# Weighted passes of a graph kernel: stored adjacency blocks replaced by stored source one-hots and a mark per slot

## What is computed

```python
def _sage_conv(x, src, dst, ea, Wl, bl, Wr):
    msg = relu(x[src] + ea)                                  # ea: edge attributes, 64 wide
    s = segment_sum(msg, dst, num_segments=N)
    cnt = segment_sum(ones, dst, num_segments=N)
    return s / maximum(cnt, 1.0)[:, None] @ Wl + bl + x @ Wr  # three of these in a row
...
def _wgin_layer(x, src, dst, edge_weight, W1, W2):
    agg = segment_sum(edge_weight[:, None] * x[src], dst, num_segments=N)
    return relu(agg @ W1.T) @ W2.T                            # two of these in a row
```

## Time and profile before

| | us |
|---|---|
| time before, median of 3 runs | 13441.07 (13429.87 to 13461.34) |
| span of the profiled execution | 17899.9 |
| first pass in it (122 to 4256) | 4134 |
| second, third pass (4367 to 5841, 5880 to 7350) | 1474, 1470 |
| weighted passes (7423 to 8222, 8277 to 9075) | 799, 798 |
| attention layers and dense parts (the rest) | about 9200 |

### The profile page before, as it was taken

How to read it: one execution, slowest core, us unless ns; L and a number is a source line. 1 busy time by engine, 2 the same in 40 slices (tenths; PEclk the granted TensorE clock), 3 DMA queues, 4 the chain that set the end, 5 groups by cost and what they waited for, 6 DMA issues and landing times. The chain is left out here.

```text
span 17899.9 us, 289186 instructions
## 1 busy us (share of the span) xinstructions
PE 11230.3 (63%) x73051; PEld 9956.4 (56%) x73052; DVE 8110.3 (45%) x22787; ACT 4549.9 (25%) x9519; POOL 8237.8 (46%) x8516
## 2 busy tenths in 40 slices
PE   5777777777878788687854444554444454455454
PEld 4666666765777677576744444443444443444443
DVE  4444444444333333300045555554555555555556
ACT  2333333333111111100012332332323232233333
POOL 3333333332444444333425555545555553555553
PEclk8777776677777777798965555555555555555555
DMA  3444444443444444465622232222222232233321
GB/s 120 136 132 132 132 134 134 134 134 101 128 122 125 116 123 123 130 209 167 210 72 71 71 72 71 74 60 62 70 71 71 70 73 51 70 74 74 72 73 48
DMA packets 1390391, 1840.09 MB, mean 103 GB/s; under 512 B 402712, under 2 KB 1116467, under 8 KB 1388954
## 3 DMA queue, kind: packets, MB, share of 16 engines
q1 hardware_dynamic: 749274, 832.66, 15.3%
q10 hardware_dynamic: 367424, 691.34, 11.8%
q0 software_dynamic: 272384, 301.97, 9.4%
HBM read 1408.99 MB, written 416.01 MB: 102 GB/s over the span
## 5 line engine op out<-in xcount | busy, mean ns | idle before, releaser
L2027 POOL DMA_INDIRECT rows<-gat_table,idx x2457 | 2357.8, 960 | 2331.1 <-DMA idx<-in_src 1527.6
L2027 POOL DMA_INDIRECT Y<-gat_table,idx x2394 | 2299.3, 960 | 1715.4 <-DMA idx<-in_src 901.5
L2059 PE MATMUL bank<-ident,scratch 8*128 8x8 f32 x1386 | 388.9, 352 | 3519.5 <-DVE scratch L2166 2249.0
L881 POOL DMA_INDIRECT bins<-scratch,slots x1288 | 1283.6, 997 | 2457.9 <-DVE slots L1146 1136.3
L2059 PEld LDWEIGHTS bank<-ident,scratch 8*128 8x128 f32 x1386 | 343.6, 306 | 3722.9 <-issue 3722.9
L893 POOL DMA_INDIRECT rows<-node_table,idx x1386 | 1361.8, 983 | 1707.6 <-DMA idx<-in_src 1316.9
L947 PE MATMUL bank<-xT 112*64 112x120 f32 (+1 forms) x11648 | 1831.9, 333 | 131.5 <-issue 130.5
L947 PEld LDWEIGHTS bank<-xT 112*64 112x64 f32 (+1 forms) x11648 | 1741.2, 183 | 179.6 <-issue 158.9
L1237 ACT ACTIVATE xT<-xT 112x256 f32<-112x256 f32 x1456 | 603.9, 415 | 3839.5 <-DVE xT L1074 2623.1
L1074 DVE TENSOR_TENSOR xT<-scores,xT 112x256 f32<-112x256 f32 x1028 | 435.0, 423 | 2431.2 <-remote 1496.7
L2086 PE MATMUL bank<-sel,msg 128*72 128x32 f32 x9702 | 1308.6, 309 | 0.0
(11 more groups left out here) (249 smaller groups left out, 21346.7 us busy)
## 6 DMA issues: line engine op xcount, KB each, us to landing
work<-in_dst_rows SPq DMA_DIRECT2D x693, 448.0 KB
work<-near_table SPq DMA_DIRECT2D x858, 224.0 KB
xT<-bins ACTq DMA_DIRECT2D x1456, 119.0 KB
adj<-work ACTq DMA_DIRECT2D x598, 240.0 KB
work<-adj ACTq DMA_DIRECT2D x184, 780.0 KB
xT<-adj ACTq DMA_DIRECT2D x184, 780.0 KB
near_table<-work SPq DMA_DIRECT2D x598, 224.0 KB
bins<-zeros ACTq DMA_DIRECT2D x46, 1547.0 KB, 7.8
```

The source lines that it names most:

```text
L881: nc.gpsimd.indirect_dma_start(bins, bass.IndirectOffsetOnAxis(slots[u % 2][:, r * G + j:r * G + j + 1], 0), binf[r][:, j, :], None).then_ ...
L2027: nc.gpsimd.indirect_dma_start(rows[s][:, j, :], None, gat_table, bass.IndirectOffsetOnAxis(idx[s % RR][:, j:j + 1], 0)).then_inc(s_rows[s ...
L2059: nc.tensor.matmul(small[:, 64:64 + H], spread_out[:, 0, :], ident[0:H, 0:H], start=True, stop=True)
```

## The change

The weighted passes no longer use adjacency blocks. `gin_pass` is gone, `sage_pass` is now `cell_pass`, and the weighted passes are `cell_pass(…, NBK, 1, weighted=True)`: they load the stored `near` (13 pieces of 224 KB per block, SP queue), fetch the node rows by it, multiply them by the weight of the slot on DVE (`weigh`), make `far_hot` on DVE, and sum by destination, with the bursts after pieces 3, 7 and 12. ACT does nothing in them. Destination place and weight of each slot come from a new small DRAM tensor `mark_table`, which the first pass fills: one ACT copy of 8 columns per piece (`mark`) and one store of 46 KB per block. The first pass loses `turned_cells`, its `weigh`, `adjacency` and `keep`, and its fetch gets the freed PSUM bank 4 as a second one.

```diff
-        adj = dram("adj", (NBK, P, TS * MW))
+        mark_table = dram("mark_table", (NBK, SL, TS * 2))
...
+        marks = [sb(f"marks{i}", [P, TS * 2]) for i in range(2)]
+        marked = [m[0:SL, :].rearrange("p (t v) -> p t v", v=2) for m in marks]
...
-            at_plain = [5] if first_pass else [1, 5, 9]
+            at_plain = [5] if first_pass else [1] if weighted else [1, 5, 9]
...
-            joint = [bank[3]] if first_pass else [bank[3], bank[4]]
+            joint = [bank[3], bank[4]]
...
+                    def marks_load(b, u):
+                        wait(sp, (q["joined"], NPC * (b - 1)))
+                        sp.dma_start(marks[u % 2][0:SL, :], mark_table[ds(b, 1), :, :].rearrange("o p f -> (o p) f")
+                                     ).then_inc(s_marks[u % 2].handle, 16)
...
-                    def adjacency(b, u, i):
-
-                        qn, k = NPC * b + i, NPC * u + i
-                        wait(pe, (q["weighed"], qn + 1), (q["far_hot_ready"], qn + 1), (q["adj_out_ready"], qn))
-                        for c in range(PC):
-                            last = nc.tensor.matmul(adj_sum[:, c * MW:(c + 1) * MW], turned[k % R][0:SL, c * P:(c + 1) * P],
-                                                    far_hot[k % RR][0:SL, c * MW:(c + 1) * MW], start=True, stop=True)
-                        last.then_inc(q["adj_ready"].handle, 1)
...
-                        wait(pe, (q["cells_ready"], qn + 1), (q["far_hot_ready"], qn + 1),
+                        wait(pe, (q["joined" if weighted else "cells_ready"], qn + 1), (q["far_hot_ready"], qn + 1),
...
+                    def weigh(qn, k, s, u, i):
+                        wait(ve, (q["fetched"], qn + 1), (q["cells_summed"], qn - RR + 1))
+                        nc.vector.tensor_tensor(cellf[s][0:SL, :, 0:D], joint[k % JR][0:SL, 0:PC * D].rearrange("p (c d) -> p c d", d=D),
+                                                bc(marked[u % 2][:, i * PC:(i + 1) * PC, 1], [SL, PC, D], 2), ALU.mult).then_inc(q["joined"].handle, 1)
...
-                    def turned_cells(qn, k, s):
-                        wait(ve, (q["adj_ready"], qn - R + 1))
-                        nc.vector.tensor_tensor(turned[k % R][0:SL, :].rearrange("p (c m) -> p c m", m=P), bc(counts[0:SL, 1:P + 1], [SL, PC, P], 1),
-                                                bc(payf[s][0:SL, :, D], [SL, PC, P], 2), ALU.is_equal).then_inc(q["turned_ready"].handle, 1)
...
-                        for c in range(PC):
-                            w = turned[k % R][0:SL, c * P:(c + 1) * P]
-                            last = nc.scalar.activation(w, w, ACT.Copy, scale=payf[s][0:SL, c, D + 2:D + 3])
-                        last.then_inc(q["weighed"].handle, 1)
...
-                        nc.scalar.activation(adj_out[s], adj_sum[:, 0:PC * MW], ACT.Copy).then_inc(q["adj_out_ready"].handle, 1)
-                        wait(ac, (q["adj_out_ready"], qn + 1))
-                        ac.dma_start(adj[ds(b, 1), :, i * PC * MW:(i + 1) * PC * MW].rearrange("o p f -> (o p) f"), adj_out[s]).then_inc(s_kept[s].handle, 16)
+                    def mark(qn, s, b, u, i):
+                        if i == 0:
+                            wait(ac, (s_marks_kept[u % 2], 16 * (b // 2) if isinstance(b, int) else 8 * (b - u % 2)))
+                        nc.scalar.activation(marked[u % 2][:, i * PC:(i + 1) * PC, :], payf[s][0:SL, :, D + 1:D + 3], ACT.Copy).then_inc(q["marked"].handle, 1)
...
-        gin_pass("gin0", node_table, X)
+        cell_pass("gin0", node_table, X, NBK, 1, weighted=True)
```

More of the change, by code:

```diff
@@ L850, in body @@
                                     aux_load(b, u, it, at_aux.index(i))
+                            if weighted and i == 3 and not (isinstance(b, int) and b == B - 1):
+                                marks_load(*after(b, u, it, 1)[:2])
                             if i in at_plain and not (isinstance(b, int) and b == B - 1):
@@ L1271, in body @@
                             if first_pass:
-                                weigh(qn, k, s)
-                                if i > 1:
-                                    keep(b, u, it, i - 2)
-                                elif not (isinstance(b, int) and b == 0):
-                                    keep(*after(b, u, it, -1), NPC + i - 2)
+                                mark(qn, s, b, u, i)
                             if not (isinstance(b, int) and qn + RR >= pieces):
                                 cells_load(*spot(b, u, it, i, RR))
+                        if first_pass:
+                            marks_keep(b, u)
                     if first_pass:
@@ L1317, in sage_pass @@
                 overflow()
-            sum_further(name, table, True, first_pass)
+            sum_further(name, table, not weighted, first_pass)
         def overflow():
```

205 lines of the change are left out of this document (59 added, 146 removed).

## The result

The changed kernel takes 13945.9 us (median of four runs, 13943.1 to 13948.0), the kernel before, timed beside it, 13435.5 us (13413.0 to 13461.3). The ratio is 1.0385, 95% interval 1.0372 to 1.0397: slower, by 510 us.

What follows compares the result with a forecast made beforehand. PE's order, with the adjacency in it, was taken to pace the first pass; 17899.9 + 1910 - 1191 = 18619 us profiled, +719 x 0.7509 = +540, a median of 13980 us; range 13420 to 14700.

Steps and rivals of the forecast that it cites:

- The weighted passes: Fetches and sums priced by the second pass: 38.1 us per block, 1754 us per pass, 1910 us added by two.
- The warm bound: Weighted-pass block at a granted clock of 1.00: 29.2 us, or 1342 us per pass.
- No stage with fetches has had over 0.78: Argument against the clock staying up in the new weighted passes, which would give 13362 us.
- The first pass: Loses the adjacency products, 971.8 us, and half the idle time before them, 220: gains 1191 us, down to 2943 us.
- my bounds of 408 and 1777: First-pass gain: 408.1 us if DVE's order paces it, 1777 us if adjacency work and both PE waits all go.
- The even factor: Conversion of the profiled execution to the median, 13441.07 / 17899.9 = 0.7509, used on all stages: +719 becomes +540 us.
- the rival of the uneven scale: Old weighted passes keep 797 us unprofiled, the rest shrinks by 0.7265: median 13527 us; chance 0.14.
- The clock falls: Clock of 0.5 in the new weighted passes and the first pass: median 15294 us; chance 0.07.
- The clock stays up: New weighted passes at 1342 us each add 1086 us, less than the first pass gives: 13362 us; chance 0.07.
- The first pass down to POOL: First pass falls until POOL is full, 44.0 us per block, gaining 2111 us: median 13290 us; chance 0.06.
- The loads don't keep up: In the weighted passes PE would wait for `near_table` before fetches; priced inside the upper bound, no chance of its own.
- PE's idle time put down to `weigh`: Sign in the weighted passes: PE's idle time before the fetch would be put down to DVE's `weigh`.

Runs made afterwards that it cites:

- before_look: The kernel before the change, without an edit, run in the slow place for a profile: 18191.3 us.
- double_fetch: The changed kernel with each fetch product of the first pass made twice, in the quick place: 14092.8 us, ratio 1.0499 to the kernel before.
- turned_back: The changed kernel with DVE's comparison of the old first pass put back, its result unused, in the slow place: 18741.9 us, ratio 1.0446 to the kernel before.
- two_adj: The kernel before with two alternating PSUM banks for the first pass's adjacency products, one for its fetch, in the quick place: 13150.8 us, ratio 0.9791.
- second_bank: The kernel before with a second PSUM bank for the fetch of its first pass, in the quick place: 13431.2 us, ratio 1.0.

## Why the prediction was right, and where its steps were off

The forecast was 13980 us; the time is 13945.9. The direction and the mechanism hold: the weighted passes add more than the first pass gives. That the total is only 34 us off is luck: both terms are far off, and their errors cancel.

**The weighted passes: right mechanism, term too large.** Forecast 1754 us each in the slow place, measured 1460 and 1480. Per block that is 31.7 us against 38.1. PE's part is 1247.5 / 46 = 27.1 us where I had 32.3, idle time 4.6 us where I had 5.8. The step that failed is the price of a product: I took it from the second pass, at a clock of 0.78, and the new passes ran at 0.86 and 0.85. A sum costs 295 ns in them and not 330, a fetch 283 and not 300. The added time was 1317 us and not 1910. The warm bound, 29.2 us per block, was no bound for the quick place: there a block takes 25.1 us, 24.3 of them PE busy at a clock of 0.96, and of the 5.8 us idle time less than 1 is left. "No stage with fetches has had over 0.78" was true of the one trace that I had, and fell by the other place, where the second pass has 0.97.

**The first pass: right mechanism, term too large as well.** Forecast 2943 us, measured 3451 in the slow place, a gain of 739 and not 1191. Three steps make up the 452 us. The first is a reading: I took the whole 971.8 us of the adjacency products off PE's busy time, though their records overlap with others'. By the trace of `before_look` PE is busy 2315 of its 3143 us with products other than these, so their removal takes 828 us and not 972 (144 us). The second is the price of what stays: 2315 us became 2537.5 (223 us), by a factor of 1.10, and the clock fell from 0.71 to 0.64, by 1.11; a fetch takes 350 ns after, 321 before. The third is idle time: it fell by 133 us, 1047 to 914, where I had half of the wait before the adjacency products, 220 (86 us). `double_fetch` shows the same link from the other side, products put back into this pass raise its clock. The gain lies between my bounds of 408 and 1777, and the pass stayed just under the 3500 us from which I had called DVE's order the bound; `turned_back` says that DVE's comparison is paid at 154 to 208 of 408 us. I had PE's order as what paces this pass: for the kernel before `two_adj` bears that out, but after the change `double_fetch` speaks against it.

**The sum and its conversion.** In the slow place both terms came short, by 452 and 593 us: +578 by stages for a forecast of +719. Converted evenly by 0.7509 the terms were -894 and +1434, +540 in sum; in the quick place -549 and +1061 came, and +510 in the medians, so that errors of 345 and 373 us cancel there. The even factor is wrong stage by stage. From the slow to the quick place the first pass shrinks to 0.71, the second to 0.66, a weighted pass to 0.77 before and 0.79 after. So the rival of the uneven scale was right that the scale is uneven, and wrong in what it did with it: it kept the old weighted passes at 797 us (625 measured) and shrank all the rest by 0.7265, the new ones to 1274 us (1154 measured). What I called "a profiled execution" against "the median" was in truth one place against another.

**The other rivals.** *The clock falls* came true in the first pass (to 0.64 in the slow place, 0.80 against 0.84 in the quick one) and not in the weighted passes, where it stayed near that of the old ones (0.88 and 0.86 in the slow place, 0.98 and 0.96 in the quick one); what stays in the first pass cost 223 us more, not thousands. The Trainium skill (TensorE: Matmul & The Clock Gate, "HAM oscillation — how this bites in real kernels") has an array that waits between bursts of products fall back to the throttled clock. The first pass agrees with it in direction: products went, most of the idle time stayed (1047 us before, 914 after), and the clock fell from 0.71 to 0.64. The weighted passes have 4.6 us idle per block and stayed at 0.86. *The clock stays up* was right on the clock of the weighted passes in the quick place (0.96), but its gain was not to be had: converted as it was, it had them add 1086 x 0.7509 = 815 us, and 1061 came, while the first pass gained only 549. *The first pass down to POOL* did not happen in the slow place, where a block takes 75.0 us. In the quick place it takes 52.9, not far above POOL's own work, which by this rival's count (busy time and the time from one DMA to the next) is 2162 / 46 = 47.0 us. *The loads don't keep up* is refuted by 14.4 us before the fetch.

**What the profile after was to show.** PE idle before the fetch of the first pass below 585 us: 88 in the slow place, 0 in the quick one. Fetches and sums each over 600 us busy: 643 and 616 in the slow place, 595 and 539 in the quick one, so this was a sign for one place only. A clock of 0.75 to 0.85: 0.85 and 0.86 in the slow place, 0.96 in the quick one, so just above it or well above it. A first pass near 2940 us: no, 3451 in the slow place, and 2434 in the quick one where 2943 x 0.7509 = 2210 would be its like. PE's idle time put down to `weigh`: wrong in the quick place (7 us), in part right in the slow one (64.5 of 216.9 us before the fetches). `near_table` below 50 us: yes. Weighted passes not below 1394 us each: 1460 and 1480 in the slow place; the 1154 us of the quick one are to be held against 1394 x 0.7509 = 1047.

**Still open.** Why one place is slower. Single instructions take the same time in both: the destination one-hots (L1069, later L1063) 651 and 649 ns, ACT's copy for relu some 0.41 us, and the DMA queue of the loads 2728 us of packets (15.0% of 18190) and 2740 (20.4% of 13431) for the same 832.66 MB. Longer are the waits, and the granted clock is lower (0.76 against 0.97 in the second pass). The clock can't be the whole cause: in the attention layers it is 0.50 in both places, a product by `ident` takes 424 ns in both, and yet 8200 us of `before_look` (9300 to 17500) hold 4529 records of it where 6300 us of `second_bank` (6700 to 13000) hold 4641, 1.33 times the time for each. What is longer there is idle time, in part such as no releaser ends: 296 us of it before one group on DVE (L2188, `work<-scores,work`) against 6. Where that comes from stays open. The 418 us of the first pass that neither the bank nor the comparison explains are not split further either.

## What to carry to other kernels

Price products by the clock that the stage will have after the edit, not by the one before: in the first pass here, taking products out lowered the clock and gave back part of the gain (0.71 to 0.64), and putting products in raised it (0.80 to 0.87). Before a group's busy time is taken off its engine's, look how much of it overlaps with other groups (here, in `before_look`, 167 of 995 us). Before work is removed for the wait that it causes, look whether another buffer removes the wait alone: here one PSUM bank for the waiting products gives 276 us with nothing recomputed, and the same bank at the fetch gives nothing, since PE then waits before the adjacency products. And check that the profile and the times come from the same place before one factor is laid over all stages.

## What the runs showed of the hardware

- The same program took 13.43 ms in one place and 17.9 to 18.2 ms in another, with equal durations of its DVE, ACT and DMA work; stages shrank to between 0.66 and 0.79, so that even the cost of the change differs by place (3.85% and 3.3%). In the attention layers the granted clock is 0.50 in both, and the slow place takes 1.33 times as long all the same.
- In the first pass 4784 more records of products cost 138 us of time for 362 us of busy time, and the clock rose from 0.80 to 0.87; in `two_adj` the same products took 185 us less of PE once a wait between them was gone (0.84 to 0.90).
- On DVE, comparing and multiplying in one instruction of 112x128 took 345 to 357 ns, four of them 1.38 to 1.43 us, where one comparison of 112x512 took 0.68 us.
